# Cross attention with normalised heads: scores of four heads in one call, exponentials first in ScalarE's steps, queries and keys turned a step earlier

## What is computed

```python
x = x + tanh(g_xattn[1]) * L1_xattn(layernorm(x), ctx, ...)

q = ln((x @ Wq + bq).reshape(b, s1, 16, 32), qn_w, qn_b)         # 16 heads of 32
k, v = split((y_main @ Wkv + bkv).reshape(b, 240, 16, 64))       # k = ln(k, kn_w, kn_b)
k_dca, v_dca = split(y_dca @ Wkv_dca + bkv_dca)                  # the last 16 keys; k_dca = ln(k_dca, ...)
ctx     = softmax(q k^T * 32**-0.5) v
ctx_dca = softmax(q k_dca^T * 32**-0.5) v_dca
out     = (ctx + ctx_dca) @ Wo + bo
```

## Time and profile before

| | us |
|---|---|
| median of three runs | 3731.67 |
| the profiled execution's own time | 3731.69 |
| its span | 3729.9 |
| regular part of the second attention, 2330 to 2918 | 588 |

### The profile page before, as it was taken

One profiled execution on the slowest core, in us unless ns is written; L12 is line 12 of the kernel. 1 busy time (PEld: TensorE's weight loads), 2 busy tenths in 40 slices (PEclk: granted clock), 3 DMA queues, 4 the chain that ended last, 5 costly groups with the idle time before them and its releaser, 6 DMA issues. The chain is left out here.

```text
span 3729.9 us, 68005 instructions
## 1 busy us (share of the span) xinstructions
PE 3581.6 (96%) x23268; PEld 3103.4 (83%) x23268; DVE 2182.2 (59%) x5411; ACT 1822.4 (49%) x4698; POOL 1531.7 (41%) x1536
## 2 busy tenths in 40 slices
PE   7999999999999998699999997999999899999999
PEld 7999999999999997699999985666666578877777
DVE  6666666556666665566666676777777542222221
ACT  4444445544444443455555544777777632222222
POOL 3333333534444443465566644766666430000000
PEclk9999999999999999899999998999999899999999
DMA  4566665316666661666666652221221120000000
GB/s 153 177 224 222 228 224 214 126 57 218 217 217 217 217 224 51 234 240 227 239 233 240 231 189 94 67 64 60 65 64 61 40 82 23 23 23 23 23 23 23
DMA packets 227766, 520.16 MB, mean 139 GB/s; under 512 B 12273, under 2 KB 28914, under 8 KB 223474
## 3 DMA queue, kind: packets, MB, share of 16 engines
q1 hardware_dynamic: 122866, 296.36, 22.8%
q10 hardware_dynamic: 94432, 187.71, 13.6%
q0 software_dynamic: 10272, 33.63, 2.7%
HBM read 266.52 MB, written 251.13 MB: 139 GB/s over the span
## 5 line engine op out<-in xcount | busy, mean ns | idle before, releaser
L672 POOL TENSOR_SCALAR a_prob<-a_prob,a_rinv 128x256 f32<-128x256 f32 x512 | 471.3, 931 | 836.0 <-DVE a_rinv L855 836.0
L619 ACT ACTIVATE a_prob<-a_prob,a_low_bias 128x256 f32<-128x256 f32 x512 | 256.5, 502 | 458.6 <-DVE a_low_bias L846 458.6
L1118 PE MATMUL e_gb<-e_xt_hi,in_hi 128*128 128x256 f32 x1248 | 354.5, 284 | 5.7 <-DVE e_xt_lo L1244 5.7
L1120 PE MATMUL e_gb<-e_xt_hi,in_lo 128*128 128x256 f32 x1248 | 354.4, 284 | 0.0
L1102 POOL TENSOR_TENSOR e_act_hi<-e_act_f,e_zeros 128x256 fp32r<-128x256 f32 x156 | 234.6, 1504 | 285.3 <-DVE e_act_f L1264 273.7
L1119 PE MATMUL e_gb<-e_xt_lo,in_hi 128*128 128x256 f32 x1248 | 351.5, 282 | 0.0
L2242 ACT ACTIVATE f_h_f<-f_hb,b_sb 128x512 f32<-128x512 f32 x128 | 88.1, 688 | 478.3 <-PE f_hb L2180 414.4
L422 PE MATMUL a_pj<-a_xt,a_wq_hi 128*128 128x256 f32 x1024 | 310.2, 303 | 0.9 <-DVE a_q_lo L705 0.9
L424 PE MATMUL a_pj<-a_xt,a_wq_lo 128*128 128x256 f32 x1024 | 289.4, 283 | 0.0
L423 PE MATMUL a_pj<-a_xt,a_wq_hi 128*128 128x256 f32 x1024 | 289.0, 282 | 0.0
L705 DVE TENSOR_TENSOR a_ot_lo<-a_avb,a_ot_hi 128x256 fp32r<-128x256 f32 x256 | 108.3, 423 | 254.4 <-ACT a_ot_hi L624 254.4
(11 more groups left out here) (362 smaller groups left out, 11370.7 us busy)
## 6 DMA issues: line engine op xcount, KB each, us to landing
raw_in<-in_w_gate SPq DMA_DIRECT2D x39, 2048.0 KB, 7.8
x_sorted<-a_blank ACTq DMA_DIRECT2D x42, 1792.0 KB, 6.5
y_sorted<-a_blank ACTq DMA_DIRECT2D x42, 1792.0 KB, 8.5
raw_out<-in_w_out SPq DMA_DIRECT2D x39, 1024.0 KB, 5.1
e_xg<-x_sorted SPq DMA_DIRECT2D x39, 512.0 KB, 8.4
y_sorted<-e_y_sb SPq DMA_DIRECT2D x39, 512.0 KB, 2.8
xt_rows<-a_xt SPq DMA_DIRECT2D x16, 1024.0 KB, 5.1
a_xt<-xt_rows SPq DMA_DIRECT2D x16, 1024.0 KB, 5.2
```

The lines of the kernel that those rows point to most:

```text
L619: e = nc.scalar.activation(prob[:, u % 4, t], prob[:, u % 4, t], ACT.Exp, bias=low_bias[:, u % 2, t:t + 1], scale=-1.0, accum_out=rsum[:, ...
L672: p = nc.gpsimd.tensor_scalar(prob[:, u % 4, t], prob[:, u % 4, t], rinv[:, u % 2, t:t + 1], None, ALU.mult)
L1118: nc.tensor.matmul(out, a_hi, b_hi, start=start, stop=False)
L1120: return nc.tensor.matmul(out, a_lo, b_hi, start=False, stop=stop)
```

## The change

Three things change in `gated_normed_attention`.

1. `scores(i, g)` now makes four heads (two pairs) at once, on four row parts and into all four banks of `sc`, once in two steps. It stands in odd steps, behind the early unit, and waits for the exponentials of both pairs before it. Its loop over queries is outside and over the four heads inside.
2. In ScalarE's steps both heads' exponentials come first; then the first copy, in even steps the high part of the values, then queries and keys, then the second copy.
3. `qk1` to `qk3` are turned one step earlier (steps 7, 1 and 3 instead of 0, 2 and 4), and their scaling moves a step earlier too. `ORDER`, and with it the bank and the predecessor of the units, changes. VectorE waits for an earlier turn before it writes the bias of odd pairs.

```diff
         for g in range(GROUPS):
-            plan(2 * g - 3, "scale", g)
-            plan(2 * g - 2, "qk", g)
+            plan(2 * g - 4 if g else -3, "scale", g)
+            plan(2 * g - 3 if g else -2, "qk", g)
...
-        ORDER = ("q0", "qk1", "q1", "qk2", "v1", "v0", "o0", "qk3", "o1", "k0", "qk0", "k1", "x0", "x1")
-        OF = {"q0": 1, "qk1": 0, ...
+        ORDER = ("q0", "q1", "qk2", "v1", "v0", "qk3", "o0", "o1", "k0", "qk0", "k1", "qk1", "x0", "x1")
+        OF = {"q0": 1, "qk1": 1, ...
...
-            def scores(i, n):
-                g, first = divmod(n, 2)
-                if first == 0:
-                    pe.wait_ge(taken["qk"], 2 * GROUPS * i + g + 1)
-                pe.wait_ge(e_done, LOOP * i + n + 1)
+            def scores(i, g):
+                pe.wait_ge(taken["qk"], 2 * GROUPS * i + g + 1)
+                pe.wait_ge(e_done, LOOP * i + 2 * g + 2)
                 for t in range(2):
-                    for j in range(2):
-                        at = (2 * first + j) * HD
-                        mm = nc.tensor.matmul(sc[:, n % 2, j, t * S:(t + 1) * S], qk[at:at + HD, g % 2, t * P:(t + 1) * P],
+                    for h in range(HG):
+                        at = h * HD
+                        mm = nc.tensor.matmul(sc[:, h // 2, h % 2, t * S:(t + 1) * S], qk[at:at + HD, g % 2, t * P:(t + 1) * P],
                                               qk[at:at + HD, g % 2, S:], start=True, stop=True)
-                mm.then_inc(s_ready, 1)
+                mm.then_inc(s_ready, 2)
...
             def step(i, u):                                    # TensorE
-                if pair(i, u + 1):
-                    scores(i, u + 1)
...
                 for bb, use, half in due(i, u, "early"):
                     unit(i, bb, use, half)
+                if u % 2 and pair(i, u + 1):
+                    scores(i, (u + 1) // 2)
                 for bb, g in due(i, u, "qk"):
                     turn_qk(i, bb, g)
...
             def step(i, u):                                    # ScalarE
-                for j in range(2):
-                    if pair(i, u):
-                        exps(i, u, j)
-                    if j == 1:
-                        (queries and keys)
-                    if pair(i, u - 2):
-                        copy_pt(i, u - 2, j)
-                    if j == 0 and u % 2 == 0 and pair(i, u - 4):
-                        (high part of the values)
+                if pair(i, u):
+                    exps(i, u)
+                if pair(i, u - 2):
+                    copy_pt(i, u - 2, 0)
+                if u % 2 == 0 and pair(i, u - 4):
+                    (high part of the values)
+                (queries and keys)
+                if pair(i, u - 2):
+                    copy_pt(i, u - 2, 1)
...
                     dve.wait_ge(s_max, N + 1)
+                    if N > 3 and n % 2:
+                        dve.wait_ge(t_ready, 2 * (N - 3))
```

More of the change, by code:

```diff
@@ L1483, in gated_normed_attention @@
         last_room = {"o0": pj[0], "o1": pj[1]}
-        ORDER = ("q0", "qk1", "q1", "qk2", "v1", "v0", "o0", "qk3", "o1", "k0", "qk0", "k1", "x0", "x1")
-        OF = {"q0": 1, "qk1": 0, "q1": 1, "qk2": 0, "v1": 1, "v0": 1, "o0": -1, "qk3": 0, "o1": -1, "k0": 2, "qk0": 1, "k1": 2, "x0": 2, "x1": 2}
+        ORDER = ("q0", "q1", "qk2", "v1", "v0", "qk3", "o0", "o1", "k0", "qk0", "k1", "qk1", "x0", "x1")
+        OF = {"q0": 1, "qk1": 1, "q1": 1, "qk2": 0, "v1": 1, "v0": 1, "o0": -1, "qk3": 0, "o1": -1, "k0": 2, "qk0": 1, "k1": 2, "x0": 2, "x1": 2}
         def room(use):
@@ L1757, in turned_ahead, with exps @@
                 nc.scalar.copy(ahead.xt_hi[:, c], sc[:, c // 2, c % 2]).then_inc(ff_xt_hid, 1)
-            def exps(i, n, j):
+            def exps(i, n):
                 p, s = prob[:, n % 4], sc[:, n % 2]
[L1761 to L1766, removed]
-                if j == 1:
-                    e.then_inc(e_done, 1)
+                act.wait_ge(s_bias, LOOP * i + n + 1)
+                nc.scalar.activation(p[:, :, :, 0:DCA], p[:, :, :, 0:DCA], ACT.Exp).then_inc(d_done, 1)
+                for j in range(2):
+                    for t in range(2):
+                        e = nc.scalar.activation(p[:, j, t, DCA:], s[:, j, t * S + DCA:(t + 1) * S], ACT.Exp, bias=nmax[:, n % 2, 1, 2 * j + t:2 * j + t + 1],
+                                                 accum_out=rsum[:, n % 4, 1, 2 * j + t:2 * j + t + 1])
+                e.then_inc(e_done, 1)
             def copy_pt(i, n, j):
@@ L1784, in step @@
                     nc.scalar.activation(sq[:], nrm[:, bb % 2, 2 * half:2 * half + 2], ACT.Square).then_inc(sq_done, 1)
-                for j in range(2):
-                    if pair(i, u):
-                        exps(i, u, j)
[L1788 to L1794, removed]
-                    if pair(i, u - 2):
-                        copy_pt(i, u - 2, j)
-                    if j == 0 and u % 2 == 0 and pair(i, u - 4):
-                        g = (u - 4) // 2
-                        act.wait_ge(av_ready, 2 * GROUPS * i + g + 1)
-                        nc.scalar.copy(ot_hi[:, g // GROUPS % 2, g % GROUPS], avb[:, 0:S]).then_inc(ot_hid, 1)
+                if pair(i, u):
[3 more added lines that the diff above has]
+                if u % 2 == 0 and pair(i, u - 4):
+                    g = (u - 4) // 2
+                    act.wait_ge(av_ready, 2 * GROUPS * i + g + 1)
+                    nc.scalar.copy(ot_hi[:, g // GROUPS % 2, g % GROUPS], avb[:, 0:S]).then_inc(ot_hid, 1)
+                for bb, g in due(i, u, "qk"):
+                    act.wait_ge(ready["qk"], GROUPS * (2 * i + bb) + g + 1)
+                    of = room(f"qk{g}")
+                    for n, cols in enumerate((slice(0, S), slice(S, S + DCA), slice(S + DCA, 2 * S))):
+                        l = nc.scalar.activation(qk[:, g % 2, cols], of[:, cols], ACT.Identity, bias=ln_sb[:, 2 * n + 1:2 * n + 2], scale=ln_sb[:, 2 * n:2 * n + 1])
+                    l.then_inc(taken["qk"], 1)
+                if pair(i, u - 2):
+                    copy_pt(i, u - 2, 1)
                 for bb, in due(i, u, "turn"):
```

## The result

The changed kernel takes 3779.9 us (median of four runs, 3777.3 to 3782.9), the kernel before 3731.1 (3730.2 to 3732.4). The ratio is 1.0131, with a 95% interval of 1.0113 to 1.0148: 49 us slower. The forecast was slower, 3813 us in a range of 3742 to 3870. So the side and the range were right, and the loss was put too high, at 82 us for 49; the likeliest case's own range (3790 to 3835) was missed. The profiled execution took 3779.5 us with a span of 3777.7.

The account below looks back on a forecast made before the run. TensorE was taken to set the pace. To 3731.7 us the forecast added 33 us for waits net of the packing's gain and 48 us for clock falls, giving 3813 us in a range of 3742 to 3870.

Parts of the forecast that it names:

- the likeliest case: Whole kernel: waits come and the clock falls about once a batch; 3813 us, own range 3790 to 3835, chance 0.48.
- What bounds the kernel: Changed stage: TensorE sets the pace, busy 565.7 of 588 us, with a period of 42.47 us a batch.
- The packing: Scores call on TensorE: four heads take 1.07 us instead of 2.13, saving 4.25 us a batch.
- the values row: TensorE's timeline before the change: values call, sixteen records on four column parts, 1.00 us; nearest row for the new call.
- does nothing: Rival, scores call: four heads still take 2.13 us; 3829 us at full clock, 3877 with falls; chance 0.05.
- The waits by order: TensorE's batch: waits rise from 2.4 to 9 us, period to 44.7, +2.2 a batch, 33 us over 15 batches.
- Edits costed at nothing: Moved turns and GpSimd scaling, DMAs, VectorE's new wait, new order of rooms: no cost; o0 possibly 1 us a batch.
- The clock: Long pause of step 2: one fall to 1.2 GHz a batch, 3.2 us each, 15 x 3.2 = 48 us.
- The waits come, the clock holds: Rival, regular part: the added waits come without falls of the clock; 3765 us; chance 0.22.
- The one on the other side: Rival: TensorE stays the bound, 4.25 us a batch kept, 3668 us; chance 0.15 including cases between it and no change.

Follow-up runs that it names:

- turn ahead only: The kernel before with only the third part, queries and keys turned a step earlier with the new order of rooms: 3739.6 us, ratio 1.0020.
- four heads only: The changed kernel with parts two and three undone, leaving only four heads' scores in one call: 3788.2 us, ratio 1.0152 to the kernel before.
- square last: The changed kernel with ScalarE's square at the end of its steps 0 and 2 instead of their head: 3739.3 us, ratio 1.0019.
- square last and k1: The changed kernel with the square at the end of ScalarE's steps and VectorE's take of k1 ahead of the maxima: 3732.6 us, ratio 1.0004.
- all three: Also "the fast version": changed kernel, square late, k1 taken ahead of maxima, queries and keys turned ahead of scores: 3689.7 us, ratio 0.9886.
- exponentials split: The changed kernel with ScalarE's old order of exponentials and copies: 3770.2 us, ratio 1.0106 to the kernel before.
- v1 in the pause: The changed kernel with v1 made ahead of step 2's second turn, in the long pause: 3763.0 us, ratio 1.0091 to the kernel before.
- two heads at a time: The changed kernel with the same four heads in one call, ordered so that two heads come before the other two: 3786.7 us, ratio 1.0144.
- k1 before the maxima: The changed kernel with VectorE's take of k1 in step 7 ahead of the maxima instead of behind them: 3768.3 us, ratio 1.0100.
- turn before scores: The changed kernel with queries and keys turned ahead of scores in odd steps and ahead of k0 in step 6: 3781.2 us, ratio 1.0133.

## Why the prediction was right, and where it was off

**What bounds the kernel.** Right: TensorE set the pace before, and in every row of the table the time follows the start-to-start period of its scores.

**The packing.** Right in size: sixteen records cost 1.07 to 1.08 us (scores at 2469.71, the next turn at 2470.78), the 1.07 that I had set by the values row. The rival "does nothing" is refuted by the row. By the Trainium skill ("TensorE: Matmul & The Clock Gate", section Measured speedup vs the span model) I had estimated 1.3 (with twice 2.13 us for one row part it is 1.4); the measurement decides for 1.07. The Trainium skill warns that packed calls move the limit to what reads PSUM ("TensorEngine Tiling (Array Packing)", section PSUM Bottleneck). The rows here don't show that: what reads PSUM became less busy (ScalarE 424.9 us of 588 instead of 461.2, VectorE 384.5 instead of 443.1); its place in the order became the limit.

**The waits by order.** Right: each of the four parts within 0.1 us, 44.7 against 44.86, and each wait where it was put. One reason was wrong: I let the turn ahead remove the 0.92 us of scores' waits, which it doesn't (turn ahead only, 0.92 still there); scores' new place does. The sum didn't depend on that. I multiplied by 15 batches (33 us); the trace has 34 us in 14 batches, 8 at the stage's beginning, which I left out, and 3 less at its end, so that this part came to some 39 us, 6 more than I had. The closeness of 0.2 us in 45 holds some luck as well: the same kind of schedule for the experiments missed by 0.03 to 1.4 us a batch.

**Edits costed at nothing.** Moved scaling, gathers, SP's loads and the new wait of VectorE: none ends a pause in the rows of the changed kernel. o0 (2498.83) did not wait for the take of v0, though that take (2497.57 to 2498.25) was over only 0.6 us ahead of it.

**The clock.** The step that failed, a term that was mis-sized: "15 x 3.2 = 48 us". It measured 10. There were seven falls in batches 1 to 14 where I had one in each, and each cost 1.3 to 1.6 us where I had 3.2. I had let TensorE run at 1.2 GHz all the way from the pause to the next scores, 3.8 us of work in 7 us; the rows show some 3.4 us at that level (2399 to 2404: clock 0.66) and the full clock again before the scores, so such a fall can cost half of 3.4 us and no more (the ones of 2.8 us in other kernels were longer). In five of the seven it lay wholly behind the pause and cost 1.6; in the other two (2581 and 2809) it began 0.6 us before the pause ended, and cost 1.3. The longest pause is the same 2.75 us in every batch, so its length alone doesn't tell in which a fall comes. The kernels with the new call whose longest pause is at most 1.9 us (four heads only, square last, square last and k1, all three; 1.87 with the exponentials split) had none in the regular part of their profiled executions (with the exponentials split, two others had a lower mean clock), and v1 in the pause (1.49) one; with 2.75 us there were seven (changed), eight (two heads at a time) or four (k1 before the maxima), and with 2.82 (turn before scores) one in every batch. So in the regular part they go with the long pause; what else decides, I leave open.

**The rivals.** "The waits come, the clock holds" (3765) stands nearer to 3780 (15 us off) than the forecast (33 off), though its condition did not hold: there were falls, one in every second batch and each at half its price, and the other 5 us are the stage's beginning and end. The one on the other side, faster at 3668 if waits stay under 6.7 us a batch, named the right condition: at 39.94 us a batch the fast version has 4.1 us of waits above 35.8 of work, and it is faster by 41 us. As a forecast of this kernel it was wrong: its waits are 9 us.

## What to carry to other kernels

When a wait is merged or moved, write down for each engine, in its order, which instruction releases the next engine, and add up the whole loop; busy shares (ScalarE 78% of the stage) say nothing about it, and a schedule from start-to-start times was right to 0.2 us in 45 here, and to 1.4 in the worst of the experiments. Work that leaves the stretch ahead of a wait uncovers that wait: the shorter TensorE stretch of step 2 made a 0.96 us square cost 41 us of the 49, 10 of them through the clock. And try fixes together: three edits that alone brought 41, 12 and -1 us brought 90 together, since each only showed the next wait.

## What the runs showed of the hardware

Records on different row parts don't seem to keep the order of the program. In the two-at-a-time kernel the program has both halves of heads 0 and 1 ahead of heads 2 and 3, but four records start within 35 ns (2488.698, 2488.705, 2488.725, 2488.731), the next four 0.32 us later, and then four every 0.215 us, nearly as in the changed kernel. The call of two heads in the kernel before starts two at a time. Windows of 50 ns at the head of a call of each kernel, the records of scores alone (length, busy us of TensorE, count, clock, DMA):

```profile
2488.69:2488.74 0.05, 0.04 (x4) 1.00 0.00 0
2511.11:2511.16 0.05, 0.04 (x2) 1.00 0.00 0
```

A record doesn't name its row part, so this is inferred: two parts start two records at once, so four at once must be on four parts, that is, records of heads 2 and 3 start with those of heads 0 and 1. Whether the engine or the compiler lets them pass, no run here shows. Either way each row part works through its own four records, and a call lasts as long as its fullest part: eight records on two parts 1.06 us, sixteen on four 1.07. The Trainium skill, "TensorE: Matmul & The Clock Gate", section The mechanism (of row and column tiling), says that matmuls keep strict program order and that only weight loads are pulled ahead; by that the call would have taken about twice as long, if the order of the program is the one that reached the engine. The starts in this trace differ from it, and the measurement decides.
